# Combining a pair's two linear maps with two full-width products in place of four half-width ones

## The chip, the cores and the metric

The kernel runs on one core of a Trainium2 chip. The metric is device time in microseconds, the median of several runs. Before the change it is 644.4 us (three runs, 644.12 to 645.06).

## What is computed

For 128 samples, each a 128 x 2048 matrix `x[b]` in float32, two conditioned linear layers with residuals are applied one after the other. The weights of each layer are picked by an integer per sample:

```python
def _L0_cond_ref(x, weights, condition):
    return jnp.einsum('bct,bcd->bdt', x, weights[condition])          # 16 maps of 128x128

def _L1_cond_ref(x, subjects, weights, biases):
    out = jnp.einsum('bct,bcd->bdt', x, weights[subjects])            # 32 maps of 128x128
    return out + jnp.transpose(biases[subjects], (0, 2, 1))

x = x + _L0_cond_ref(x, L0_cond_weights, itok_B_0_15)
x = x + _L1_cond_ref(x, itok_B_0_31, L1_cond_weights, L1_cond_biases)
```

So each output is (I + W1)^T (I + W0)^T x + bias, and the two 128 x 128 maps can be multiplied into one before x is touched. x and the output are 134 MB each.

## The kernel before

Samples are taken in 64 pairs, k = 0 and 1 being the two samples of a pair. A sample's 128 rows lie on 64 partitions, two rows (u = 0 and 1) behind each other on a partition, so that sample 0 fills partitions 0 to 63 and sample 1 partitions 64 to 127, and a pair is one 2 MB transfer each way with 16 KB runs. `xt` has 8 slots of one pair each. Results are written back into the slot and stored from there.

**Queues.** SP issues the loads: the two weight tables, then the 64 pair loads (line 111), each of them from the ninth on waiting until the store of its slot has landed. ACT issues the 64 stores (line 262). These are the only large transfers.

**POOL** (lines 125 to 139) forms, for each sample, `map0T` = transposed W0 + I (line 137) and `map1` = W1 + I (line 138). Both tiles have two buffers, one per pair in turn; from pair 2 on POOL waits for the combining of two pairs before.

**PE** (lines 141 to 206). `combine` (line 151) multiplies the two maps of each sample of a pair: four products with 64 weight columns and 128 moving columns, for k = 0, 1 and u = 0, 1, which put sample k's result on partitions 64k to 64k + 63 of columns 1536 to 1791 of `acc1`, the first half of its last bank. `pair` then multiplies the combined map, copied to `both`, with x: 16 products (`term`, line 159) of 512 columns on 64 rows, alternately of sample 0 into `acc0` and of sample 1 into `acc1`, over four blocks j = 0 to 3 of 512 columns. The combining for the next pair is issued in the middle of a pair, between blocks 1 and 2; block 3 of `acc1` uses the bank in which the combined maps lie, and waits for `both_ready` before it. PE's program has the first eight pairs written out, then a loop over six groups of eight, then the last eight written out. Each float32 product is two matmul instructions and two weight loads in the trace.

**DVE** (lines 222 and 224) takes sample 0's results out of `acc0` with the bias added, in halves of 1024 columns, **ACT** (line 247, `odd_out`) sample 1's out of `acc1`. Between its first and second `odd_out` of a pair ACT does `copy_maps` for the next pair (line 240): one 128 x 256 copy of the combined maps to `both`. The order of ACT's work in a pair is: odd_out, copy_maps, odd_out, then two more odd_outs and the store's issue. PE waits for `lo_out0`, `lo_out1`, `hi_out0` and `hi_out1` (results taken out) before it writes the same banks for the next pair.

Of the kernel before, what the change touches and what calls it, by code (L numbers as in the profile page):

```python
# [5 lines left out]
def conditioned_residual_kernel(  # L6
# [12 lines left out]
    ALU = mybir.AluOpType  # L19
    ACT = mybir.ActivationFunctionType  # L20
    POOL = mybir.EngineType.Pool

    B, C, T = x.shape
    S0, S1 = w0T.shape[1], w1.shape[1]
    HC = C // 2
# [13 lines left out]
    with ctx:  # L39
        def sb(name, shape, dt=fp32):  # L40
            return ctx.enter_context(nc.sbuf_tensor(name, shape, dt))

        def pb(name, shape):
            return ctx.enter_context(nc.psum_tensor(name, shape, fp32))
# [15 lines left out]
        map0T = sb("map0T", [C, 2, 2, 2, HC])  # L60
        map1 = sb("map1", [C, 2, 2, 2, HC])
        both = sb("both", [C, 2, 2, C])
# [3 lines left out]
        acc1 = pb("acc1", [C, T])  # L66

        CB = T - CHUNK
# [16 lines left out]
        both_ready = sem("both_ready")  # L85
# [11 lines left out]
        w0T_v = w0T_sb[:, :, :].rearrange("p s (i u) -> p s u i", u=2)  # L97
        w1_v = w1_sb[:, :, :].rearrange("p s (i u) -> p s u i", u=2)
        ident_v = ident[:, :].rearrange("p (i u) -> p u i", u=2)
# [13 lines left out]
        @block.gpsimd  # L113
        def _(pool):
            nc.gpsimd.memset(ident[:, :], 0.0).then_inc(zeroed, 1)  # L115
            nc.gpsimd.iota(row[:, :], [[0, B]], base=0, channel_multiplier=1).then_inc(row_ready, 1)  # L116
            pool.wait_ge(zeroed, 1)
            nc.gpsimd.affine_select(out=ident[:, :], in_=ident[:, :], compare_op=ALU.not_equal, fill=1.0, base=0,  # L118
                                    pattern=[[-1, C]], channel_multiplier=1).then_inc(ident_ready, 1)
            pool.wait_ge(ident_ready, 1)  # L120
            pool.wait_ge(cond_loaded, LOAD)
            pool.wait_ge(w0_loaded, LOAD)
            pool.wait_ge(w1_loaded, LOAD)
            GROUP = 16
            for b in range(B):
                if b % GROUP == 0:
                    _, i0 = nc.values_load_multi_w_load_instructions(  # L127
                        cond_sb[0:1, 0, b:b + GROUP], engines=[POOL], min_val=0, max_val=S0 - 1,
                        skip_runtime_bounds_check_because="conditions index the maps")
                    _, i1 = nc.values_load_multi_w_load_instructions(  # L130
                        cond_sb[0:1, 1, b:b + GROUP], engines=[POOL], min_val=0, max_val=S1 - 1,
                        skip_runtime_bounds_check_because="conditions index the maps")
                q, k = b // 2, b % 2
                if q >= 2 and k == 0:

                    pool.wait_ge(combined, q - 1)
                nc.gpsimd.tensor_tensor(map0T[:, q % 2, k, :, :], w0T_v[:, bass.ds(i0[b % GROUP], 1), :, :], ident_v, ALU.add)  # L137
                nc.gpsimd.tensor_tensor(map1[:, q % 2, k, :, :], w1_v[:, bass.ds(i1[b % GROUP], 1), :, :], ident_v,  # L138
                                        ALU.add).then_inc(maps_ready, 1)

        @block.tensor
        def _(pe):

            pe.wait_ge(bias_loaded, LOAD)
            pe.wait_ge(ident_ready, 1)
            nc.tensor.matmul(acc0[0:S1, 0:C], bias_sb[:, :], ident[:, :], start=True, stop=True).then_inc(turned, 1)  # L146
            pe.wait_ge(onehot_ready, 1)
            pe.wait_ge(biasT_ready, 1)
            nc.tensor.matmul(acc1[:, 0:B], biasT[:, :, :], onehot[:, :], start=True, stop=True).then_inc(picked, 1)  # L149

            def combine(q, buf):
                pe.wait_ge(maps_ready, 2 * q + 2)
                for k in range(2):
                    for u in range(2):
                        last = nc.tensor.matmul(acc1[k * HC:(k + 1) * HC, CB + u * C:CB + (u + 1) * C],  # L155
                                                map0T[:, buf, k, u, :], map1[:, buf, k, :, :], start=True, stop=True)
                last.then_inc(combined, 1)

            def term(acc, k, u, buf, slot, j):
                return nc.tensor.matmul(acc[:, j * CHUNK:(j + 1) * CHUNK], both[k * HC:(k + 1) * HC, buf, u, :],  # L160
                                        xt[k * HC:(k + 1) * HC, slot, u * T + j * CHUNK:u * T + (j + 1) * CHUNK],
                                        start=u == 0, stop=u == 1)

            def pair(q, slot, turn, begins, ends):
                buf = slot % 2
                pe.wait_ge(x_loaded[slot], (turn + 1) * LOAD)
                pe.wait_ge(both_ready, q + 1)
                if not begins:
                    pe.wait_ge(lo_out0, q)
                term(acc0, 0, 0, buf, slot, 0)  # L170
                if not begins:
                    pe.wait_ge(lo_out1, q)
                term(acc1, 1, 0, buf, slot, 0)
                term(acc0, 0, 1, buf, slot, 0)
                term(acc1, 1, 1, buf, slot, 0)
                term(acc0, 0, 0, buf, slot, 1)
                term(acc1, 1, 0, buf, slot, 1)
                term(acc0, 0, 1, buf, slot, 1).then_inc(lo_done0, 1)
                term(acc1, 1, 1, buf, slot, 1).then_inc(lo_done1, 1)
                if not begins:  # L180
                    pe.wait_ge(hi_out1, q)
                if not ends:
                    combine(q + 1, 1 - buf)
                if not begins:
                    pe.wait_ge(hi_out0, q)
                term(acc0, 0, 0, buf, slot, 2)
                term(acc1, 1, 0, buf, slot, 2)
                term(acc0, 0, 1, buf, slot, 2)
                term(acc1, 1, 1, buf, slot, 2)
                term(acc0, 0, 0, buf, slot, 3)  # L190
                if not ends:

                    pe.wait_ge(both_ready, q + 2)
                term(acc1, 1, 0, buf, slot, 3)
                term(acc0, 0, 1, buf, slot, 3).then_inc(hi_done0, 1)
                term(acc1, 1, 1, buf, slot, 3).then_inc(hi_done1, 1)

            def group(turn, begins, ends):
                for s in range(SLOTS):
                    pair(turn * SLOTS + s, s, turn, begins and s == 0, ends and s == SLOTS - 1)  # L200

            pe.wait_ge(bias_ready, 1)
            combine(0, 0)
            group(0, True, False)
            with pe.Fori(1, TURNS - 1) as turn:
                group(turn, False, False)
            group(TURNS - 1, False, True)
# [25 lines left out]
        @block.scalar  # L233
        def _(act):
            act.dma_start(cond_sb[:, :, :], conds).then_inc(cond_loaded, LOAD)
            act.dma_start(bias_sb[:, :], bias1).then_inc(bias_loaded, LOAD)
            act.dma_start(cond_rep[:, :], conds[0:1, 1, :].to_broadcast([S1, B])).then_inc(rep_loaded, LOAD)
            act.wait_ge(bias_ready, 1)

            def copy_maps(q):  # L240

                act.wait_ge(combined, q + 1)
                nc.scalar.activation(both[:, q % 2, :, :], acc1[:, CB:CB + 2 * C], ACT.Identity).then_inc(both_ready, 1)  # L243

            def odd_out(q, v, a):

                return nc.scalar.activation(xt[HC:C, q % SLOTS, v * T + a:v * T + a + HALF], acc1[v * HC:(v + 1) * HC, a:a + HALF],  # L247
                                            ACT.Identity, bias=bias_of[v * HC:(v + 1) * HC, 2 * q + 1:2 * q + 2])

            copy_maps(0)  # L250
            for q in range(PAIRS):
                act.wait_ge(lo_done1, q + 1)
                odd_out(q, 0, 0)
                if q < PAIRS - 1:
                    copy_maps(q + 1)
                odd_out(q, 1, 0).then_inc(lo_out1, 1)
                act.wait_ge(hi_done1, q + 1)
                odd_out(q, 0, HALF)
                odd_out(q, 1, HALF).then_inc(hi_out1, 1)
                act.wait_ge(hi_out0, q + 1)  # L260
                act.wait_ge(hi_out1, q + 1)
                act.dma_start(out_pairs[q, :, :], xt[:, q % SLOTS, :]).then_inc(stored[q % SLOTS], LOAD)
            for q in range(SLOTS):
                act.wait_ge(stored[q], LOAD * TURNS)
# [27 lines left out]
```

## Time and profile before

| what | value |
|---|---|
| median of three runs | 644.4 us |
| profiled execution: own time / span | 643.72 us / 641.6 us |
| granted TensorE clock, mean | 0.964 |
| PE busy | 525.4 us (82%) |
| PE weight loads busy | 224.2 us (35%) |
| DVE, ACT, POOL busy | 329.2, 309.4, 124.1 us |
| DMA moved | 271.82 MB, mean 424 GB/s |

The own time is what the execution took on the device; the span goes from its first to its last instruction. "Busy" is the time in which at least one instruction of an engine ran. The clock is the share of full speed that TensorE was granted. The 271.82 MB are x in, the result out, and about 3.4 MB of weights, instructions and small tables. The page's row of DMA share in 40 slices reads 8 in the first slice, 9 (90% or more) in 38 and 5 in the last.

### The profile page before, as it was taken

The page shows a single profiled execution, that of the slowest core. Times are in us where ns is not written, and L with a number is a line of the kernel's source. Part 1 is how long each engine was busy: PE and PEld are TensorE (multiplying, and loading weights), DVE is VectorE, ACT ScalarE, POOL GpSimd, SP SyncE. Part 2 cuts the span into 40 slices and gives each one's busy share as a digit, 9 for nine tenths or more (in the row PEclk, how much of TensorE's full clock was granted, in tenths as well). Part 3 has the DMA queues.
Part 4 walks back from the last instruction along what each step waited for, and adds up shares of the span by engine and source line. Part 5 has one row for each costly group of instructions (what it writes and reads, how often), then busy time and mean ns, then how long its engine had stood idle before and what let it go on. Part 6 is the DMA issues. An engine that isn't in the chain of part 4 may idle for free.

```text
span 641.6 us, 6679 instructions
## 1 busy us (share of the span) xinstructions
PE 525.4 (82%) x2564; PEld 224.2 (35%) x2564; DVE 329.2 (51%) x259; ACT 309.4 (48%) x321; POOL 124.1 (19%) x263
## 2 busy tenths in 40 slices
PE   1899999887787787887888977889878888779880
PEld 0344443333333333333333433333333333334330
DVE  0366666455545544554546445455554545455450
ACT  0466665444544544544446445355454445454450
POOL 2222222121221221221212212122112122121000
PEclk9999999899999999999989899899999889998896
DMA  8999999999999999999999999999999999999995
GB/s 361 436 396 434 429 430 431 428 433 430 429 431 432 433 431 430 430 430 434 429 431 431 430 433 431 430 432 430 431 431 431 432 431 429 431 431 431 430 430 246
DMA packets 18931, 271.82 MB, mean 424 GB/s; under 512 B 2241, under 2 KB 2274, under 8 KB 2274
## 3 DMA queue, kind: packets, MB, share of 16 engines
q1 hardware_dynamic: 9504, 137.37, 50.3%
q10 hardware_dynamic: 9410, 134.26, 48.9%
q8 instruction: 7, 0.11, 0.1%
q14 instruction: 10, 0.08, 0.0%
HBM read 137.40 MB, written 134.22 MB: 423 GB/s over the span
## 4 chain that ended last, share of the span: by engine, by line
DMA 75%; PE 19%; DVE 3%; ACT 1%; POOLq 0%; issue 0%; DVEq 0%; POOL 0%; SPq 0%; ACTq 0%
DMA out_dram<-xt 40%; DMA xt<-in_x_dram 33%; PE acc L160 17%; PE acc L155 1%; DMA w_sb<-in_w_dram 1%; DVE xt L222 1%; DVE xt L224 1%; ACT xt L247 0%; DVEq L39 0%; ACT L243 0%; POOLq L127 0%; POOLq L130 0%; POOL map0T L137 0%; POOL map L138 0%; ACT both L243 0%
## 5 line engine op out<-in xcount | busy, mean ns | idle before, releaser
L160 PE MATMUL acc<-xt,both 64*128 64x512 f32 x2048 | 489.8, 621 | 85.2 <-DMA xt<-in_x_dram 83.2
L247 ACT ACTIVATE xt<-acc,bias_of 64x1024 f32<-64x1024 f32 x256 | 283.6, 1108 | 300.2 <-PE acc L160 297.8
L160 PEld LDWEIGHTS acc<-xt,both 64*128 64x128 f32 x2048 | 196.2, 193 | 336.7 <-issue 223.5
L222 DVE TENSOR_SCALAR xt<-acc,bias_of 64x1024 f32<-64x1024 f32 x128 | 163.3, 1276 | 282.1 <-PE acc L160 282.1
L224 DVE TENSOR_SCALAR xt<-acc,bias_of 64x1024 f32<-64x1024 f32 x128 | 165.1, 1290 | 1.9
L137 POOL TENSOR_TENSOR map0T<-w0T_sb,ident 128x128 f32<-128x128 f32 x128 | 65.6, 512 | 469.6 <-PE acc L155 457.8
L138 POOL TENSOR_TENSOR map<-w_sb,ident 128x128 f32<-128x128 f32 x128 | 65.7, 513 | 0.0
L155 PEld LDWEIGHTS acc<-map,map0T 128*64 128x64 f32 x512 | 27.4, 137 | 49.3 <-issue 48.1
L155 PE MATMUL acc<-map,map0T 128*64 128x128 f32 x512 | 43.0, 287 | 0.9 <-POOL map L138 0.9
L243 ACT ACTIVATE both<-acc 128x256 f32<-128x256 f32 x64 | 24.5, 383 | 0.8
L146 PE MATMUL acc<-ident,bias_sb 128*32 128x128 f32 x2 | 0.6, 422 | 10.7 <-DMA bias_sb<-in_bias_dram 10.7
L243 ACT ACT_TABLE_LOAD x1 | 1.3, 1283 | 16.4 <-PE acc L155 16.4
L213 DVE TENSOR_TENSOR onehot<-cond_rep,row 32x128 f32<-32x128 int32 x1 | 0.3, 280 | 12.9 <-DMA cond_rep<-in_conds_dram 12.9
L146 PEld LDWEIGHTS acc<-ident,bias_sb 128*32 128x32 f32 x2 | 0.2, 142 | 10.7 <-DMA bias_sb<-in_bias_dram 10.7
L149 PE MATMUL acc<-onehot,biasT 32*128 32x128 f32 x2 | 0.8, 480 | 2.2 <-DVE biasT L215 2.2
L149 PEld LDWEIGHTS acc<-onehot,biasT 32*128 32x128 f32 x2 | 0.5, 304 | 2.6 <-DVE onehot L213 2.6
L217 DVE COPY bias_of<-acc 128x128 f32<-128x128 f32 x1 | 0.3, 291 | 0.9 <-PE acc L149 0.9
L215 DVE COPY biasT<-acc 32x128 f32<-32x128 f32 x1 | 0.3, 279 | 0.0
L118 POOL TENSOR_SCALAR_AFFINE_SELECT ident<-ident 128x128 f32<-128x128 f32 x1 | 0.3, 282 | 0.0
L115 POOL MEMSET ident<- 128x128 f32 x1 | 0.2, 204 | 0.3 <-POOLq L281 0.3
L116 POOL IOTA row<- 32x128 int32 x1 | 0.2, 224 | 0.0
L281 POOL MEMSET const-float32-0.0<- 128x1 f32 x1 | 0.1, 98 | 0.2 <-issue 0.2
(3 smaller groups left out, 0.3 us busy)
## 6 DMA issues: line engine op xcount, KB each, us to landing
xt<-in_x_dram SPq DMA_DIRECT2D x64, 2048.0 KB, 30.7
out_dram<-xt ACTq DMA_DIRECT2D x64, 2048.0 KB, 37.2
w_sb<-in_w_dram SPq DMA_DIRECT2D x1, 2048.0 KB, 9.4
w0T_sb<-in_w0T_dram SPq DMA_DIRECT2D x1, 1024.0 KB, 4.8
cond_sb<-in_conds_dram ACTq DMA_DIRECT2D x1, 1.0 KB
bias_sb<-in_bias_dram ACTq DMA_DIRECT2D x1, 16.0 KB, 9.4
cond_rep<-in_conds_dram ACTq DMA_DIRECT2D x1, 16.0 KB, 11.1
```

The lines of the kernel that those rows point to most:

```text
L118: nc.gpsimd.affine_select(out=ident[:, :], in_=ident[:, :], compare_op=ALU.not_equal, fill=1.0, base=0, pattern=[[-1, C]], channel_multipl ...
L137: nc.gpsimd.tensor_tensor(map0T[:, q % 2, k, :, :], w0T_v[:, bass.ds(i0[b % GROUP], 1), :, :], ident_v, ALU.add)
L138: nc.gpsimd.tensor_tensor(map1[:, q % 2, k, :, :], w1_v[:, bass.ds(i1[b % GROUP], 1), :, :], ident_v, ALU.add).then_inc(maps_ready, 1)
L146: nc.tensor.matmul(acc0[0:S1, 0:C], bias_sb[:, :], ident[:, :], start=True, stop=True).then_inc(turned, 1)
L149: nc.tensor.matmul(acc1[:, 0:B], biasT[:, :, :], onehot[:, :], start=True, stop=True).then_inc(picked, 1)
L155: last = nc.tensor.matmul(acc1[k * HC:(k + 1) * HC, CB + u * C:CB + (u + 1) * C], map0T[:, buf, k, u, :], map1[:, buf, k, :, :], start=Tru ...
L160: return nc.tensor.matmul(acc[:, j * CHUNK:(j + 1) * CHUNK], both[k * HC:(k + 1) * HC, buf, u, :], xt[k * HC:(k + 1) * HC, slot, u * T + j ...
L213: nc.vector.tensor_tensor(onehot[:, :], cond_rep[:, :], row[:, :], ALU.is_equal).then_inc(onehot_ready, 1)
L222: nc.vector.tensor_scalar(xt[0:HC, q % SLOTS, a:a + HALF], acc0[0:HC, a:a + HALF], bias_of[0:HC, 2 * q:2 * q + 1], None, ALU.add)
L224: return nc.vector.tensor_scalar(xt[0:HC, q % SLOTS, T + a:T + a + HALF], acc0[HC:C, a:a + HALF], bias_of[HC:C, 2 * q:2 * q + 1], None, AL ...
L243: nc.scalar.activation(both[:, q % 2, :, :], acc1[:, CB:CB + 2 * C], ACT.Identity).then_inc(both_ready, 1)
L247: return nc.scalar.activation(xt[HC:C, q % SLOTS, v * T + a:v * T + a + HALF], acc1[v * HC:(v + 1) * HC, a:a + HALF], ACT.Identity, bias=b ...
```

## The change

`combine` makes two products in place of four. Each has 128 weight columns (both samples' rows of one u, side by side) and 256 moving columns (both samples' columns). The result has four blocks, of which the two crossed ones (rows of one sample with columns of the other) are not used. It fills all 512 columns of `acc1`'s last bank. `map0T` is laid out with u ahead of k for it, so line 137 writes two separate runs of 64 columns. `copy_maps` copies the two wanted blocks, sample 0's from partitions 0 to 63 and sample 1's from partitions 64 to 127, in two instructions of 64 partitions x 256 elements. The wait at a pair's start for `both_ready` is left out except in the very first pair; the wait ahead of block 3 of the pair before covers it.

```diff
-                nc.gpsimd.tensor_tensor(map0T[:, q % 2, k, :, :], w0T_v[:, bass.ds(i0[b % GROUP], 1), :, :], ident_v, ALU.add)
+                nc.gpsimd.tensor_tensor(map0T[:, q % 2, :, k, :], w0T_v[:, bass.ds(i0[b % GROUP], 1), :, :], ident_v, ALU.add)
...
             def combine(q, buf):
+
                 pe.wait_ge(maps_ready, 2 * q + 2)
-                for k in range(2):
-                    for u in range(2):
-                        last = nc.tensor.matmul(acc1[k * HC:(k + 1) * HC, CB + u * C:CB + (u + 1) * C],
-                                                map0T[:, buf, k, u, :], map1[:, buf, k, :, :], start=True, stop=True)
+                for u in range(2):
+                    last = nc.tensor.matmul(acc1[:, CB + u * 2 * C:CB + (u + 1) * 2 * C],
+                                            map0T[:, buf, u, :, :], map1[:, buf, :, :, :], start=True, stop=True)
                 last.then_inc(combined, 1)
...
                 pe.wait_ge(x_loaded[slot], (turn + 1) * LOAD)
-                pe.wait_ge(both_ready, q + 1)
-                if not begins:
+                if begins:
+                    pe.wait_ge(both_ready, 1)
+                else:
+
                     pe.wait_ge(lo_out0, q)
...
                 act.wait_ge(combined, q + 1)
-                nc.scalar.activation(both[:, q % 2, :, :], acc1[:, CB:CB + 2 * C], ACT.Identity).then_inc(both_ready, 1)
+                crossed = acc1[:, CB:T].rearrange("p (u k c) -> p u k c", u=2, k=2)
+                nc.scalar.activation(both[0:HC, q % 2, :, :], crossed[0:HC, :, 0, :], ACT.Identity)
+                nc.scalar.activation(both[HC:C, q % 2, :, :], crossed[HC:C, :, 1, :], ACT.Identity).then_inc(both_ready, 1)
```

## Rows read from the trace of the kernel before

**Rows 1.** Windows: stretch, length; busy us (instructions) per engine; clock, DMA share, GB/s.

```profile
14.00:84.00 70.00, 67.21 (x344) 30.39 (x345) 41.16 (x33) 40.18 (x42) 20.23 (x43) 1.00 1.00 423
150.00:540.00 390.00, 326.27 (x1584) 138.01 (x1586) 204.66 (x160) 192.03 (x200) 77.13 (x160) 0.97 1.01 431
```

**Rows 2.** The chain that ended last, whole span: shares, then pieces (start, us, what).

```profile
by line: DMA out_dram<-xt 39.7%; DMA xt<-in_x_dram 33.4%; PE acc L160 17.1%; PE acc L155 1.5%; DMA w_sb<-in_w_dram 1.5%; DVE xt L222 1.4%; DVE xt L224 1.2%; issue 0.4%; ACT xt L247 0.3%; DVEq L39 0.2%; ACT L243 0.2%; POOLq L127 0.2%; POOLq 
...
15.23 1.14 PE acc L155 x8
...
23.71 0.59 PE acc L155 x8
24.31 7.07 PE acc L160 x32
...
84.27 31.18 DMA out_dram<-xt
```

**Rows 3.** Stores issued in 30:31, 84:85 and 627:628, last number us to landing.

```profile
out_dram<-xt ACTq DMA_DIRECT2D x1, 2048.0 KB, 15.9
...
out_dram<-xt ACTq DMA_DIRECT2D x1, 2048.0 KB, 31.2
...
out_dram<-xt ACTq DMA_DIRECT2D x1, 2048.0 KB, 14.0
```

**Rows 4.** Waits (total us, times, longest): first of 84:560, second of 14:84.

```profile
PE acc L160 <- DMA xt<-in_x_dram: 75.2, 46, 2.4
...
PE acc L160 <- ACT both L243: 1.9, 1, 1.9
```

**Rows 5.** Groups by line: busy, mean ns, then idle before, with its releaser.

```profile
L155 PE MATMUL acc<-map,map0T 128*64 128x128 f32 x512 | 43.0, 287 | 0.9 <-POOL map L138 0.9
```

**Rows 6.** Timeline 28:46, a pair that PE paces: start, us, instruction, idle before.

```profile
31.30 0.66 PE L155 MATMUL acc<-map,map0T 128*64 128x128 f32 x8
...
31.45 1.11 ACT L247 ACTIVATE xt<-acc,bias_of 64x1024 f32<-64x1024 f32 x1 [1.20 <-PE acc L160]
...
32.17 0.51 POOL L137 TENSOR_TENSOR map0T<-w0T_sb,ident 128x128 f32<-128x128 f32 x1 [5.74 <-PE acc L155]
32.57 0.38 ACT L243 ACTIVATE both<-acc 128x256 f32<-128x256 f32 x1
...
32.98 1.11 ACT L247 ACTIVATE xt<-acc,bias_of 64x1024 f32<-64x1024 f32 x1
...
35.68 2.23 ACT L247 ACTIVATE xt<-acc,bias_of 64x1024 f32<-64x1024 f32 x2 [1.59 <-PE acc L160]
```

**Rows 7.** Timeline 0:30, around the first pair's start.

```profile
17.74 0.38 ACT L243 ACTIVATE both<-acc 128x256 f32<-128x256 f32 x1
...
18.27 5.44 PE L160 MATMUL acc<-xt,both 64*128 64x512 f32 x16 [1.91 <-ACT both L243]
```

**Rows 8.** Timeline 605:645, the last pair: its products and its store's issue.

```profile
617.32 7.14 PE L160 MATMUL acc<-xt,both 64*128 64x512 f32 x32 [1.95 <-DMA xt<-in_x_dram]
...
627.10 0.34 ACTq L262 DMA_DIRECT2D out_dram<-xt  x1
```

**Rows 9.** DMA queues (packets, MB, share): the page; 88:89; 150:540; 635.9:641.6.

```profile
q8 instruction: 7, 0.11, 0.1%
...
q8 instruction: 1, 0.02, 6.0%
...
q14 instruction: 6, 0.05, 0.0%
...
q10 hardware_dynamic: 8, 0.11, 4.7%
```

**Rows 10.** Windows between two instruction fetches, and from the last of them on.

```profile
562.40:591.80 29.40, 25.39 (x122) 10.60 (x120) 15.28 (x13) 14.33 (x16) 5.77 (x12) 0.94 1.01 430
...
591.80:626.00 34.20, 28.63 (x134) 11.84 (x130) 19.18 (x16) 17.88 (x19) 1.93 (x4) 0.95 1.01 431
```

## The prediction

> **What bounds the kernel now.** I read the windows first [rows 1]. The reader is to see the last two columns: from 14 to 84 us the share of the 16 DMA engines is 1.00 at 423 GB/s, from 150 to 540 us 1.01 at 431 GB/s. There is no stretch in the body in which the transfers stand still. PE is busy for 326 of the 390 us, but that is no bound: in the same stretch its 1584 products are 39.6 pairs of 40 (32 of line 160, 8 of line 155), so a pair takes 390 / 39.6 = 9.85 us, and a pair is 4.19 MB, which at 431 GB/s is 9.73 us. PE needs only 0.59 + 7.07 = 7.66 us for a pair when nothing holds it [rows 2], and 9.85 - 7.66 = 2.19 us per pair are over. Where they go the waits show: PE stands 75.2 us for loads of x between 84 and 560 us, and no other wait of PE's data on another engine is in that list; POOL, DVE and ACT wait for PE [rows 4, 6].
>
> The chain of waits, read second, seems to say otherwise for the start: 17.1% of it is line 160 and 1.5% line 155, because from 15 to 84 us it runs through PE alone, a combining of 0.59 us and then 7.07 us of products, pair after pair, into the store issued at 84.27 us, which takes 31.18 us to land [rows 2]. The third view settles which is right: the store issued at 30.6 us takes 15.9 us to land, the one at 84.3 us 31.2 us [rows 3]. Alone, 2.1 MB at 430 GB/s would be 4.9 us. So 11 us of other transfers stand ahead of or beside the first store, and 26 us beside the eighth: already while PE sets the pace, a backlog of transfers grows. The end of the run is the end of the bytes: total bytes over a rate that is always used. A PE or ACT cost shows in the time only if it empties this backlog, or if it lies behind the last load.
>
> **The products.** Removed: four products of 64 weight columns by 128 moving columns, eight instructions, 0.59 us from start to the next line's start [rows 2, 5]. Added: two products with 128 weight columns by 256 moving columns, four instructions, if float32 is still split in two. What one costs: line 160 does 32 instructions of 512 columns in 7.07 us, two at a time on the two halves of the rows, so a step of 512 columns is 7.07 / 16 = 0.44 us [rows 2], and 256 columns 0.22 us. I assume that nothing runs beside a product that takes the whole array, so 4 x 0.22 = 0.88 us: +0.29 us a pair. Ends: below, two of them beside each other, 0.44 us (-0.15); above, at half the clock, 1.76 us (+1.17), since the first pair's first half takes 5.44 us in place of 3.7 although the column of the clock reads 1.00 [rows 1, 7]. I take +0.29 us, by the nearest row at speed. It is hidden by the 2.19 us for which PE waits for loads; even the upper end fits. With the cover gone it would be 63 x 0.29 = 18 us.
>
> The Trainium skill speaks against this edit. TensorEngine Tiling (Array Packing), section Key Properties, has different tiles execute weight loads and products in parallel, so the old form, in 64-column tiles, could overlap its two samples, and the new one can't. The trace agrees in part: eight instructions of 128 columns one by one would be 8 x 0.11 = 0.88 us, and they take 0.59. By the rule at its fullest the old form would be 0.44 us and the change +0.44 us a pair; the sum is the same, since that too is under the 2.19 us.
>
> **The copies.** Removed: one 128 x 256 copy of 0.38 us. Added: two of 64 x 256, as many elements on each partition. From the start of the old copy to the next instruction's start is 32.98 - 32.57 = 0.41 us [rows 6], so I take 0.41 each: +0.41 us. Ends: nothing gained or lost beneath 0 (half the partitions for half the price, +0), and above the 1.11 us of the 64 x 1024 activation on the same partitions (+1.11 - 0.41 = 0.70 more). Queued behind it on ACT is the pair's second odd_out, whose end lets PE begin the next pair in acc1: it would end at 32.98 + 0.41 + 1.11 = 34.50 us, and ACT's next work comes at 35.68 [rows 6]. 1.2 us are over, and the upper end fits too. PE waits for the copies itself ahead of block 3 of acc1: it gets there one combining and four steps of 0.44 us after the combining's start, 31.30 + 0.88 + 1.77 = 33.95 us, with the weight load one step sooner, 33.5 us. The copies begin when odd_out ends (32.57, with the combining long done at 31.30 + 0.88 = 32.18) and end at 32.57 + 0.41 + 0.38 = 33.36 us. So 0.15 us are over; by the upper end PE would lose some 0.6 us a pair, and 0.6 + 0.29 is still under 2.19 us. By +1.17 and +0.6 together it would be 1.8 us, just under.
>
> **POOL's line 137** writes two runs in place of one. It costs 0.51 us, and POOL stands idle for 5.74 us before each pair even when PE paces [rows 6]; between +0 and twice the price, +1.0 us a pair, it is hidden.
>
> **The wait left out** goes with one that stays (block 3 of the pair before waits for the same copies). PE never stood at a pair's start for these maps except at 18.27 us [rows 4, 7], which wait stays. 0 us, and at most one instruction less a pair.
>
> **The head.** The combining for pair 0 takes 1.14 us there [rows 2]; times 0.88 / 0.59 it is 1.70, +0.56 us. The second copy adds 0.41, so pair 0 begins 1.0 us later. Eight combinings with +0.29 us follow by 84 us: the eighth store is issued 1.0 + 2.3 = 3.3 us later. What hides it is the backlog, 11 us at the first store and more at each later one [rows 3]. With all upper ends together the delay would be 1.0 + 8 x 1.8 = 15 us at the eighth store, where the backlog is 26.
>
> **The tail.** After the last load landed (617.3 us) the last pair has no combining and no copy; it takes 7.14 us of products, its store is issued at 627.10 and lands 14.0 us later [rows 3, 8]. Its own 4.9 us of bytes are the smaller part of that: the queue is full to the end. Untouched: 0.
>
> **Instruction fetches** are a term of their own, because the very end belongs to one DMA engine. Between 635.9 and 641.6 us only 8 packets move, one behind the other, 4.7% of 16 engines [rows 9]: fifteen engines are done, and one is some 5 us late. Equal shares of x lie on all, so it had other work. The queue q8 brought 7 packets of 16 KB, at 6.0% of 16 engines in 1 us, 0.96 us each [rows 9]; 7 x 0.96 = 6.7 us is about the lateness, if they lie on this engine, which the trace doesn't name. They fit PE's program: one comes with every 122 + 120 = 242 products and weight loads [rows 10], and none between 150 and 540 us, where PE loops and only q14 fetches [rows 9]. The change takes 8 of a pair's 80 such instructions away, 24 times in the program as written, 192 in all, and up to 24 waits. After the last of the seven fetches 134 + 130 = 264 are left [rows 10]. 264 - 192 - 24 = 48: the seventh fetch moves toward the end but still comes, in the last pair. So 0 us, with -0.96 if it falls away. ACT gets 64 instructions more, at most one more of q14's packets, which are 8 KB (0.05 MB for 6), half the size: +0.5 us as the upper end, 0 taken.
>
> The Trainium skill, Runtime: NRT & Kernel Launch, section Instruction fetch mechanics, says that a refill brings 256 instructions and that a taken branch out of a two-page window forces a fetch. The first half agrees with the 242 (waits not counted). By the second half each of the loop's turns would fetch, and a shorter body would save some; the trace shows no packet of q8 in five turns, so the trace decides and the sum has no such term.
>
> **Sum.** 641.6 us of span + 0 = 641.6; own time 643.72 + 0. The median of the runs shown is 0.7 us above that own time, so I forecast the median itself, **644.4 us**.
>
> **Rivals.**
> A. One fetch of PE's program falls away, and the late engine's end with it: 644.4 - 0.96 = 643.4 us. For it: the margin is only 48 instructions. Against: it is positive, and other steps than these may set the late engine. 0.12.
> B. More than that comes off the late engine (two fetches, or the packets fall more evenly): 644.4 - 1.9 = 642.5 us, the faster case. Nothing in the count speaks for two. 0.05.
> C. The head sets the end, as the chain of waits shows it, because the backlog runs dry when the stores come later: 644.4 + 3.3 = 647.7 us. It decides from the point where a store's delay is over the 11 us of other transfers beside the first store [rows 3]. Against: 3.3 us is far under that, and the share is 1.00 from 14 us on [rows 1]. This is the slower case. 0.05.
> D. The products don't come out as I think (split otherwise, or at half the clock) and PE needs up to 1.8 us more a pair. Under 2.19 us the time stays 644.4; 0.06. It would be slower only beyond: each 0.1 us over that is 6 us. 0.02.
> My forecast as it stands: 0.70.
>
> **How the numbers follow.** A measurement of this kernel can tell about 0.2%, 1.3 us, from no change: 643.1 to 645.7. The forecast, A and the first part of D lie inside, 0.87 (0.01 of A falls under 643.1). Faster: that and B, 0.06. Slower: C and the second part of D, 0.07. The range reaches down past A to 643.2, and up by the 0.66 us by which the highest of the runs shown lies over the median and the 0.5 us of q14, rounded, to 645.4.
>
> **What would show each step.** Line 155 with 256 matmul instructions in place of 512, 0.88 us from a combining's start to the next products; if 0.6, the old form gained nothing from its tiles. Two copies at line 243, 0.41 us apart. PE's wait for loads of x down by about 0.29 us a pair, some 14 us over 84:560, and the pair still 9.85 us. The store at 30.6 us issued 1 to 1.6 us later, and the eighth some 3 us later and landing in less time than 31.2 us, at the same 46.5 and 115.5 us or so. q8 with 7 packets before the end, the last near 618 us. The forecast is wrong if the DMA share falls under 1 anywhere between 14 and 634 us, or if PE waits for ACT's copies in the loop by over 1.5 us a pair.

## The result: 1.85 us faster, and the profile after

The kernel after takes 642.49 us (8 runs, 642.28 to 643.22), the kernel before in the same comparison 644.34 us (8 runs, 643.42 to 645.06): a ratio of 0.9973, 95% interval 0.9964 to 0.9981. A second timing of the unchanged kernel after, on another chip, gave 642.70 us and 0.9980 (0.9969 to 0.9990). I had forecast 644.4 us, range 643.2 to 645.4; the measured median lies under that range.

First the page of the kernel after; groups by line have busy us, mean ns, then idle before. They answer to the table of before and to [rows 5].

```profile
span 641.1 us, 6225 instructions
...
L160 PE MATMUL acc<-xt,both 64*128 64x512 f32 x2048 | 471.7, 602 | 70.6 <-DMA xt<-in_x_dram 68.2
...
L155 PE MATMUL acc<-map,map0T 128*128 128x256 f32 x256 | 73.3, 409 | 0.9 <-POOL map L138 0.9
...
L247 ACT ACTIVATE both<-acc 64x256 f32<-64x256 f32 x64 | 24.2, 378 | 0.7
L246 ACT ACTIVATE both<-acc 64x256 f32<-64x256 f32 x64 | 24.1, 377 | 0.7
```

The instruction count fell from 6679 to 6225: 512 of PE's away, 64 of ACT's more, and the wait's register work. Line 155 has 256 matmul instructions, as foreseen. The mean granted TensorE clock is 0.989, against 0.964 before, and one instruction of line 160 takes 602 ns on average, against 621.

The timeline of a pair that PE paces, against [rows 6] (start, us, instruction, idle before):

```profile
32.27 0.36 ACTq L266 DMA_DIRECT2D out_dram<-xt  x1
...
32.99 1.13 PE L155 MATMUL acc<-map,map0T 128*128 128x256 f32 x4
...
34.05 7.14 PE L160 MATMUL acc<-xt,both 64*128 64x512 f32 x32
34.25 0.38 ACT L246 ACTIVATE both<-acc 64x256 f32<-64x256 f32 x1
34.30 0.51 POOL L137 TENSOR_TENSOR map0T<-w0T_sb,ident 128x128 f32<-128x128 f32 x1 [6.20 <-PE acc L155]
...
34.64 0.38 ACT L247 ACTIVATE both<-acc 64x256 f32<-64x256 f32 x1
...
35.04 1.11 ACT L251 ACTIVATE xt<-acc,bias_of 64x1024 f32<-64x1024 f32 x1
```

The combining takes 34.05 - 32.99 = 1.06 us from its start to the next products', against 0.59 [rows 2]. The two copies start 0.39 us apart. POOL's line 137 takes 0.51 us as before. PE's pair is 1.06 + 7.07 = 8.13 us, against 7.66 [rows 2]. So PE became slower, and the kernel faster.

Windows (busy us and counts of PE, weight loads, DVE, ACT, POOL; clock, DMA share, GB/s) and the wait for loads in 84:560, against [rows 1, 4]:

```profile
14.00:84.00 70.00, 66.85 (x284) 30.68 (x285) 38.34 (x31) 40.40 (x49) 19.26 (x41) 1.00 1.01 426
150.00:540.00 390.00, 333.20 (x1431) 142.80 (x1427) 202.65 (x158) 204.83 (x237) 75.47 (x157) 1.00 1.01 431
```

```profile
PE acc L160 <- DMA xt<-in_x_dram: 59.6, 42, 1.5
```

The transfers run at the same 431 GB/s; PE waits 59.6 us for loads in place of 75.2, as its slower pair eats into that idle time. (The combining's 0.47 us more in some 49 pairs would be 23 us; the long products, faster at the higher clock, give part of it back.) The chain of waits gives PE even more of the span than before, in pieces of 7.07 us up to the ninth combining, and the eighth store, issued at 89.17 us in place of 84.27, lands after 27.0 us in place of 31.2 [rows 2, 3]:

```profile
by line: DMA out_dram<-xt 42.1%; DMA xt<-in_x_dram 29.6%; PE acc L160 17.1%; PE acc L155 2.6%; DVE xt L224 1.6%; DMA w_sb<-in_w_dram 1.5%; DVE xt L226 1.4%; issue 0.3%; DVEq L39 0.2%; ACT L246 0.2%; POOLq L127 0.2%; POOLq L130 0.2%; POOL ma
...
89.17 26.99 DMA out_dram<-xt
```

It lands at 116.2 us, before 115.5: of a delay of 4.9 us, 4.2 were absorbed by the backlog. Nothing in the middle of the run tells of a gain. The end does. DMA queues (packets, MB, share) of the page, and of 635.9:641:

```profile
q8 instruction: 7, 0.11, 0.1%
...
q10 hardware_dynamic: 7, 0.10, 4.5%
```

Again one engine alone moves the last packets, one behind the other, after the other fifteen are done.

**How late this engine is, and since when.** Each transfer of x ends with 16 small completion packets, one for each DMA engine. The packets' records in the trace hold the start of each; they don't name the engine, so "the sixteenth" below is the one that completes last. For every load I took how much later the last of its 16 completions came than the first; the rows of the 15th give the same for the last but one:

```
load landing near (us)     94    211    327    444    561    last data packet ends
before, last behind first  2.1   2.7    3.9    5.4    6.8    640.7
after                      1.9   2.2    3.5    4.7    6.0    640.1 (span 641.1)
the 15th, before           2.1   2.5    2.5    2.5    2.5    635.7
the 15th, after            1.4   1.9    1.9    2.3    2.6    635.5
```

The first completions of the loads come 9.725 us apart in both kernels, and the other fourteen engines stay near the first. The sixteenth falls back a little with every pair from the start on; a line through the loads that land between 280 and 600 us gives 116.5 ns a pair before and 102.4 after. Over 65 pairs that is 14 x 65 = 0.9 us. A second trace of the unchanged kernel before gave 135.0 ns a pair, second and third traces of the kernel after and of a near copy 100.8 and 100.6, so the difference is 14 to 34 ns, 0.9 to 2.2 us, and the 1.85 us lie inside. The time between span and own time is 1.8 us in nearly all runs of all kernels, so the gain isn't there. Over the 15 traces without the last store and the 32 memsets of the table below, the last data packet ends the later the steeper this slope is: 638.7 us at 92 ns, 639.4 to 640.1 at 101 to 102, 641.4 to 641.7 at 135 to 137, with a correlation of 0.95 and a rise of 0.056 us for each ns a pair, what 56 of the 64 pairs would give.

This lateness also sets PE's pair. A load is there for PE when its last completion has come, so PE's pair is 9.725 + 0.116 = 9.84 us before and 9.725 + 0.102 = 9.83 after. The chains of waits show it in the starts of PE's products eight pairs apart, first before (78.7 us), then after (78.6 us):

```profile
459.87 3.70 PE acc L160 x16
...
538.58 3.70 PE acc L160 x16
```

```profile
457.72 3.70 PE acc L160 x16
...
536.32 3.70 PE acc L160 x16
```

**Where the lateness comes from, packet by packet.** A data packet of 16 KB is recorded with 611 ns. Between 150 and 540 us some 11 of a pair's 256 are recorded a little longer, mostly by 1 to 30 ns, and these additions sum to 109 ns a pair before and 101 after, near the two slopes. I cut the stretch into slots of 607 ns and counted the instructions that end in each:

```
instructions that end in the slot        0     1-4   5-8   9-12  13 and more
mean addition in ns, before              2.2   3.7   7.3   9.5   15.2 (44 slots)
after                                    1.5   4.3   6.8   8.8   10.3 (7 slots)
after + 24 PE instructions a pair        4.7   7.2   6.0   7.1   17.9 (55 slots)
```

The additions fall where many instructions end; in all 17 traces the two are correlated, by 0.22 to 0.43. Of the 44 crowded slots before, 39 hold the old combining, whose eight products and eight weight loads run within 0.66 us; the new combining makes no such slot. If these packets are the late engine's, as their sum suggests, this shows when it is held up, though not by what.

### The profile page after: what moved, and what is told of

Same layout as the page of the kernel before. It is cut to its first block, busy times and chain, and to the rows that moved or that the text cites. A ratio compares the mean times of both kernels' runs of the same rounds, so it can differ in the third digit from the quotient of the medians.

```text
span 641.1 us, 6225 instructions
## 1 busy us (share of the span) xinstructions
PE 537.6 (84%) x2308; PEld 234.0 (37%) x2308; DVE 329.2 (51%) x259; ACT 333.2 (52%) x385; POOL 123.9 (19%) x263
## 4 chain that ended last, share of the span: by engine, by line
DMA 73%; PE 20%; DVE 3%; POOLq 0%; issue 0%; ACT 0%; DVEq 0%; POOL 0%; SPq 0%; ACTq 0%
DMA out_dram<-xt 42%; DMA xt<-in_x_dram 30%; PE acc L160 17%; PE acc L155 3%; DVE xt L224 2%; DMA w_sb<-in_w_dram 1%; DVE xt L226 1%; DVEq L39 0%; ACT L246 0%; POOLq L127 0%; POOLq L130 0%; POOL map0T L137 0%; POOL map L138 0%; ACT both L247 0%; ACT both L246 0%
## 5 line engine op out<-in xcount | busy, mean ns | idle before, releaser
L160 PE MATMUL acc<-xt,both 64*128 64x512 f32 x2048 | 471.7, 602 | 70.6 <-DMA xt<-in_x_dram 68.2
L160 PEld LDWEIGHTS acc<-xt,both 64*128 64x128 f32 x2048 | 189.5, 187 | 321.5 <-issue 224.1
L155 PE MATMUL acc<-map,map0T 128*128 128x256 f32 x256 | 73.3, 409 | 0.9 <-POOL map L138 0.9
L155 PEld LDWEIGHTS acc<-map,map0T 128*128 128x128 f32 x256 | 43.8, 191 | 52.3 <-issue 47.8
L247 ACT ACTIVATE both<-acc 64x256 f32<-64x256 f32 x64 | 24.2, 378 | 0.7
L246 ACT ACTIVATE both<-acc 64x256 f32<-64x256 f32 x64 | 24.1, 377 | 0.7
```

The source lines that it names most:

```text
L155: last = nc.tensor.matmul(acc1[:, CB + u * 2 * C:CB + (u + 1) * 2 * C], map0T[:, buf, u, :, :], map1[:, buf, :, :, :], start=True, stop=True)
L246: nc.scalar.activation(both[0:HC, q % 2, :, :], crossed[0:HC, :, 0, :], ACT.Identity)
L247: nc.scalar.activation(both[HC:C, q % 2, :, :], crossed[HC:C, :, 1, :], ACT.Identity).then_inc(both_ready, 1)
```

## The experiments

All times are medians, with the ratio of the run to the kernel before on the same chip (the ratios go nearly by the means, so they and the medians can differ by 0.1%; the medians of the kernel before on the four chips are 644.1 to 644.3 us). "ns a pair" is the slope just described, of one profiled execution each; it scatters by some 20 ns for old-form kernels.

```
kernel                                    us       ratio, 95% interval       instr.  ns a pair
before, again                             643.64   0.9990 (0.9980, 0.9999)   6679    135.0
two copies alone                          644.52   1.0001 (0.9992, 1.0009)   6743    136.5
wait left out alone                       643.41   0.9989 (0.9980, 0.9998)   6673    137.4
two products and copies, wait kept        642.63   0.9976 (0.9966, 0.9986)   6231    100.6
after                                     642.49   0.9973 (0.9964, 0.9981)   6225    102.4
after, again                              642.70   0.9980 (0.9969, 0.9990)   6225    100.8
after + 8 PE instructions a pair          643.60   1.0000 (0.9990, 1.0009)   6737    117.8
after + 24 PE instructions a pair         643.93   1.0005 (0.9993, 1.0018)   7761    119.6
after + 8 DVE instructions a pair         643.70   0.9994 (0.9984, 1.0003)   6737    120.7
after + 32 DVE instructions a pair        652.74   1.0135 (1.0115, 1.0154)   8273    -
after, half of x's products               641.67   0.9958 (0.9944, 0.9973)   4177    92.3
before, PE's loop written out             643.94   0.9997 (0.9987, 1.0006)   6606    112.9
before, half of the combining products    643.50   0.9988 (0.9980, 0.9997)   6175    107.4
before, maps formed for two pairs only    643.53   0.9991 (0.9977, 1.0004)   6169    101.6
the same, again                           643.63   0.9989 (0.9981, 0.9998)   6169    127.0
after, last store cut in two              646.57   1.0034 (1.0022, 1.0047)   6226    104.4
```

### Which part of the change

The kernel before, against itself:

> The kernel before, unchanged, timed against itself. Every theory expects a ratio of 1.000 with an interval of about 0.1% on both sides; the point is to see how far the spans of its executions scatter and how much of a time lies outside the span (2.1 us in the profiled execution of before, 1.8 us in that of after).

0.9990 with an interval that just leaves 1 out. So a single ratio here can't be trusted to better than 0.1%, 0.6 us; the gain of 0.27% is clear of that, a third of it isn't. The spans of the kernel before run from 641.1 to 643.9 us over some 30 executions, those of the kernel after from 640.4 to 641.4 with one at 643.5.

The two copies alone:

```diff
-                nc.scalar.activation(both[:, q % 2, :, :], acc1[:, CB:CB + 2 * C], ACT.Identity).then_inc(both_ready, 1)
+                nc.scalar.activation(both[0:HC, q % 2, :, :], acc1[0:HC, CB:CB + 2 * C], ACT.Identity)
+                nc.scalar.activation(both[HC:C, q % 2, :, :], acc1[HC:C, CB:CB + 2 * C], ACT.Identity).then_inc(both_ready, 1)
```

> The kernel before with its one 128x256 copy of the combined maps made as two of 64x256; four products and all waits as before. Theory F (the gain comes from PE's shorter program: its instruction fetches, which share the DMA engine that ends last): no gain, 644.3 us, ratio 0.999 to 1.001, and q8 fetches at the same times as before. Theory T (the later and more even rhythm of ACT's work, and with it the stores, gives the gain): most of the 1.85 us, 642.5 to 643.0 us.

644.52 us: no gain. Theory T fell.

The wait left out alone:

```diff
-                pe.wait_ge(both_ready, q + 1)
-                if not begins:
+                if begins:
+                    pe.wait_ge(both_ready, 1)
+                else:
                     pe.wait_ge(lo_out0, q)
```

> The kernel before with the wait for both_ready at a pair's start left out in all but the first pair. Theory F: at most one instruction a pair less on PE, 24 in its program, so at most a small part: 643.9 to 644.4 us. Theory W (the wait left out is the gain): 642.5 us. Theory T: 644.3 us.

0.9989, the same as before against itself: nothing that can be told from no change.

The kernel after with that wait put back (the same lines the other way round):

> The kernel after with the wait for both_ready at a pair's start put back: two products and two copies remain. Theory F: nearly the whole gain, 642.5 to 642.9 us, since 192 of PE's instructions stay away. Theory W: 644.3 us. Theory T: 642.5 us.

642.63 us, the whole gain. It goes with the two products; the wait isn't needed for it, and neither the copies nor the wait alone are enough. (Two products without the two copies weren't run; the new layout asks for both.)

### Is it PE's program, fetched?

The kernel before with PE's loop written out:

```diff
-            with pe.Fori(1, TURNS - 1) as turn:
-                group(turn, False, False)
+            for turn in range(1, TURNS - 1):
+                group(turn, False, False)
```

> The kernel before with PE's loop written out: the same products and waits, but 5 x 8 pairs x 83 = 3320 more instructions in the program, 13 more packets of 16 KB on q8 at 0.96 us. Theory F, all of q8 on the engine that ends last: 644.3 + 12.5 = 656.8 us. If q8's packets are spread over the engines: under 645.1 us. Theory N: the instructions executed fall by some 170 (the loop's register work), 643.6 us, plus whatever theory F adds.

643.94 us. The queue of the fetches in 150:540 (no packet before, [rows 9]):

```profile
q8 instruction: 13, 0.21, 0.2%
```

Thirteen packets more, and no time. In the completions the reason is seen: one time this engine, the next time that one falls back by 0.6 to 0.7 us, until eight of them are 2.8 to 5 us behind the first, and the engine that ends last is none the later (112.9 ns a pair, last data at 640.5 us). PE's fetches are spread over the engines. That struck out the term on which my count of the end was built.

DVE's are not. The kernel after with memsets on DVE, eight or 32 of one column behind the first output of every pair:

```diff
                 even_out(q, 0).then_inc(lo_out0, 1)
+                for i in range(32):   # 8 in the smaller one
+                    nc.vector.memset(spare[:, 32 * q + i:32 * q + i + 1], 0.0)
```

> The kernel after with eight memsets of one column each on DVE behind the first output of every pair, 512 instructions more on an engine that waits 280 us for PE. Theory N with any engine's instructions alike: 642.5 + 2.1 = 644.6 us. Theory N with PE's alone: 642.5 us. Theory F: 512 instructions are four packets of 8 KB (0.31 us each) on q14: 643.7 us if all lie on the late engine.

643.70 us. The second latest engine fell back in jumps of 0.85 us, some 104 us apart (q14's packets at 241.4, 348.6, 452.2 and 556.4 us), which is DVE's rhythm of 128 instructions at 12 a pair; the latest went on smoothly, at 120.7 ns a pair. This jump sized the next:

> The kernel after with 32 memsets of one column on DVE a pair, 2048 instructions more, all in DVE's program. Theory N, proportional: 102 + 32 x 1.1 = 137 ns a pair on the late engine, 2.3 us, 644.8 us. Theory N, flattening as with 24 more on PE: 643.9 us. Besides, q14 would fetch DVE's program in 16 more packets; with eight memsets a pair the second latest engine fell back by 0.86 us with each of DVE's fetches, so with 32 this engine would fall back by 16 x 0.86 = 14 us and end last: 635 + 2.8 + 14 = 652 us.

652.74 us, against 652 worked out. The page's span, DVE's group and queue, then the windows 635:641 and 643:649:

```profile
span 650.0 us, 8273 instructions
...
q14 instruction: 26, 0.21, 0.1%
...
L234 DVE MEMSET spare<- 128x1 f32 x2048 | 30.9, 59 | 0.6 <-issue 0.2
```

```profile
635.00:641.00 6.00, 0.00 (x0) 0.00 (x0) 0.52 (x1) 0.21 (x1) 0.00 (x0) 0.73 0.84 360
643.00:649.00 6.00, 0.00 (x0) 0.00 (x0) 0.00 (x0) 0.00 (x0) 0.00 (x0) 0.50 0.07 30
```

The memsets cost DVE 30.9 us in all, 0.5 us a pair, far under its idle time; what costs 10 us is 16 packets of 8 KB more on q14. From 644.3 us on one engine alone still stores (0.07 of 16 is one engine): its last data packet ends at 649.2 us, where fourteen others had ended by 641.5. That the engine which ends last sets the time, with all others done, is shown by this one most plainly. The fourteen themselves ended some 6 us later than in the kernel after (635.5); I put that down to the loads, which land only when the slowest engine has brought its rows, so that stores start later. No run tests this alone. The small additions to the packets sum to 141 ns a pair here.

### Is it the number of instructions executed, or the form of the product?

Tiny products of 32 weight columns by one moving column ahead of each combining, two or six of them:

```diff
                 pe.wait_ge(maps_ready, 2 * q + 2)
+                for _ in range(2):   # 6 in the larger one
+                    nc.tensor.matmul(acc1[0:32, CB:CB + 1], map0T[:, buf, 0, 0, 0:32], map1[:, buf, 0, 0, 0:1], start=True, stop=True)
```

> The kernel after with two tiny extra products ahead of each combining (32 weight columns by one moving column, 8 instructions, overwritten by the real ones): PE executes and holds about as many instructions as in the kernel before, in the new form of the product. Theory N (one DMA engine carries a small load that grows with the number of instructions executed; it is the engine whose packets end last): back to 644.0 to 644.5 us, and the lag of this engine behind the others grows by some 4.5 us between 190 and 540 us, in place of 3.8. Theory M (the full-width product itself, its time or its clock, is the gain): 642.5 us as the kernel after.

> The kernel after with six tiny extra products ahead of each combining, 24 instructions a pair, 1536 in all. Theory N, by 1.85 us for the 454 instructions that the change took away (4 ns each): 642.5 + 6.3 = 648.8 us. Theory F (only fetched program counts: 24 x 24 = 576 instructions more in the program, two and a quarter packets of 16 KB): 642.5 + 2.2 = 644.7 us. Theory M: 642.5 us, as long as PE's pair stays under 9.85 us.

643.60 and 643.93 us. The two groups of tiny products, first of the smaller one, then of the larger:

```profile
L155 PE MATMUL acc<-map,map0T 128*32 128x1 f32 x256 | 18.4, 175 | 0.7 <-POOL map L138 0.7
```

```profile
L155 PE MATMUL acc<-map,map0T 128*32 128x1 f32 x768 | 34.7, 172 | 0.8 <-POOL map L138 0.8
```

With as many instructions as before, 1.1 of the 1.85 us are gone, in the new form of the product, at the same high granted clock (0.989) as after; by the ratio, 1.0000, the whole gain is gone. So theory M, the form or the clock alone, falls. But three times the addition takes only 0.3 us more, and 119.6 ns a pair: proportional, as I had written it (648.8 us), the effect is not. Theory F's 644.7 us for this one falls too, as after the written-out loop it must. Eight on DVE (643.70 us) did the same as eight on PE.

The other direction, a kernel with half of x's products left out:

```diff
-                term(acc0, 0, 1, buf, slot, 0)
-                term(acc1, 1, 1, buf, slot, 0)
...
-                                        start=u == 0, stop=u == 1)
+                                        start=True, stop=True)
```

> The kernel after with the products of u = 1 left out (half of the sum over x's rows is missing): 32 instructions fewer a pair, 64 in place of 96. PE's pair falls to some 4.4 us, the transfers are the same. Theory N: the late engine falls back by about 64 x 1.1 = 70 ns a pair in place of 102, 65 x 0.032 = 2.1 us less at the end: 640.4 us. Any theory in which instructions don't count: 642.5 us. The floor is where the other engines end, 635 us plus 2.8 us, 637.9 us.

641.67 us and 92.3 ns a pair: faster, though by 0.8 us against after in place of 2.1, and at a lower granted clock (0.857). PE waits 198 us for loads in it:

```profile
L160 PE MATMUL acc<-xt,both 64*128 64x512 f32 x1024 | 320.9, 742 | 200.4 <-DMA xt<-in_x_dram 198.1
```

Fifteen engines end at 635.4 us, as in the kernel after (635.5); the sixteenth ends at 638.7 in place of 640.1. So it is again this engine that makes the difference.

Then as many instructions away as the change takes, in the old form, once on PE and once on POOL:

```diff
-                for k in range(2):
+                for k in range(2 if isinstance(q, int) and q == 0 else 1):
```

> The kernel before, old half-width form, with sample 1's two combining products left out in all pairs but the first (sample 1 gets wrong maps): 8 PE instructions fewer a pair, 504 in all, as the change takes away. Theory N (the number of executed instructions loads one DMA engine steadily): 642.4 to 642.8 us, late engine 100 to 104 ns a pair behind. Theory M (the full-width form is the gain): 644.2 us, 116 to 137 ns.

```diff
-            for b in range(B):
+            for b in range(4):
...
-                if q >= 2 and k == 0:
-                    pool.wait_ge(combined, q - 1)
...
-                pe.wait_ge(maps_ready, 2 * q + 2)
+                pe.wait_ge(maps_ready, 4)
```

> The kernel before with its four half-width products, but POOL forms the maps of the first two pairs only, and all pairs are combined from these two buffers (the weights of the later samples are left out, so the output is another one). Some 500 instructions fewer are executed, on POOL in place of PE. Theory N (a steady load on one DMA engine that follows the number of executed instructions of any engine): as the kernel after, 642.3 to 642.7 us, and this engine falls back by some 100 ns a pair in place of 116 to 137. Theory M (the full-width product is the gain) or N with PE's instructions alone: 644.1 us.

> The kernel before without POOL's map forming after pair 1 again, since its first 12 runs spread from 641.95 to 645.93 us. Theory N with any engine's instructions: 642.4 to 642.8 us. Theory N with PE's alone, or M: 644.2 us.

643.50, 643.53 and 643.63 us, ratios of 0.9988 to 0.9991: each lower than before, none clearly by more than before against itself (0.9990), and all about 1 us above the kernel after. So fewer instructions in the old form give at most half of the gain, where the theory asked for all of it. The slopes, 107.4, 101.6 and 127.0 ns, contradict each other; a single trace is too little for a difference of 20 ns.

> The kernel after, unchanged, again, on the chip of the other three. Every theory: 642.5 us, late engine 100 to 104 ns a pair behind. If it comes out over 643.4 us, the gain of 1.85 us is in part a matter of chip or hour.

642.70 us: the gain itself stands, on a chip on which these did not reach it.

### Taking bytes off the late engine

```diff
+                if q < PAIRS - 1:
+                    act.dma_start(out_pairs[q, :, :], ...)
+            q = PAIRS - 1
+            act.dma_start(out_pairs[q, 0:120, :], xt[0:120, q % SLOTS, :]).then_inc(stored[q % SLOTS], LOAD)
+            act.dma_start(out_pairs[q, 120:128, :], xt[120:128, q % SLOTS, :]).then_inc(stored[q % SLOTS], LOAD)
```

> The kernel after with the last pair's store cut in two: rows 0 to 119, which by the Trainium skill (DMA: Bandwidth & Descriptors, Why a DMA increments its semaphore by 16 and not by 1) lie on 15 of the 16 engines, and rows 120 to 127 on 8. If the late engine is the sixteenth, it has 8 packets fewer at the end, 8 x 0.607 = 4.9 us, and the time is 642.5 - 4.9 + what the two transfers cost, 637.6 to 638.5 us. If it is one of the other fifteen: 642.5 to 643.7 us.

646.57 us, worse than either case that I had written. Windows 627:638 and 638:645:

```profile
627.00:638.00 11.00, 0.00 (x0) 0.00 (x0) 0.00 (x0) 0.00 (x0) 0.00 (x0) 0.50 0.78 270
638.00:645.00 7.00, 0.00 (x0) 0.00 (x0) 0.00 (x0) 0.00 (x0) 0.00 (x0) 0.50 0.06 26
```

The last engine ends some 4 us later than in the kernel after, its last packet at 644.3 us in place of 640.1. Its records stand end to end: eight packets from 638.87 us, a completion, one more packet, a completion. So the engine that ends last has its share of the 120 rows and one packet of the other eight; it isn't the one that a store of 120 rows leaves out. The records count 15 + 8 completions for the two stores, as the Trainium skill has it on the page DMA: Bandwidth & Descriptors, section Why a DMA increments its semaphore by 16 and not by 1. The second store's packet is 0.6 us of the delay. The rest came before: of the data packets that start after 624 us, 37 took 0.7 to 2.6 us in place of 0.61, together 26 us more than at 0.611 us each, and none did so in the kernel after. So this store in two parts is itself slower, why isn't known, and the run can't tell what fewer bytes on the late engine would have given. Which version would relieve the late engine stays open; no kernel that beats the one after and computes the same was found.

## Why the prediction was wrong

**Right.** The bound: transfers, full from start to end, with PE's and ACT's costs hidden. The combining was mis-sized (1.06 us against 0.88, so +0.47 us a pair in place of +0.29), and the eighth store came 4.9 us later in place of 3.3. The two cost nothing, as argued, by PE's idle time and by the backlog. Rival C, the head's chain of waits, had its delay and more, and the time fell: the chain was no bound there. The copies (0.39 us apart for 0.41), POOL's 0.51 us, q8's seven packets before the end: as forecast, the last at 610 us in place of 618. PE's wait (15.6 us less for "some 14") agrees in part by luck: the combining took more than forecast, and the granted clock rose from 0.964 to 0.989, which I hadn't forecast, and made the long products faster.

**The step that failed** is the one headed instruction fetches. I had seen that the end belongs to one DMA engine, some 5 us late, and put its lateness down to "the queue q8 brought 7 packets of 16 KB", 7 x 0.96 = 6.7 us, "if they lie on this engine, which the trace doesn't name". They don't: 13 more of them cost no time, and seven in both kernels went with 1.85 us of difference. The lateness grows by 100 to 137 ns with every pair, also from 150 to 540 us, where there is no packet of q8 [rows 9]; I had that row, and should have asked whether the lateness grows there. The trace did hold the answer, in the completions, before any run. So did my first paragraph, with 9.85 us for a pair and 9.73 us for its bytes: the 0.12 us between them is what the sixteenth engine loses with every pair, and "total bytes over a rate that is always used" describes the other fifteen, which end 5 us sooner. What came was rival B, "more than that comes off the late engine", 642.5 us, to which I gave 0.05 since "nothing in the count speaks for two" fetches. Its size was right by luck, for its mechanism, fetches, was not what happened.

**What takes their place.** Shown: the engine that ends last sets the time; it falls back steadily; in the kernels with the two products it does so by less; neither the copies nor the wait alone bring the gain, and it stays when the wait is put back; 512 instructions put back on PE or on DVE bring back 1.1 to 1.2 us of the 1.85 by the medians; packets are stretched most where many instructions end, in sum by as much as that engine falls back. Not shown: what the steady load on that engine is. It rises with the instructions executed, but not in proportion (in the new form 92, 102, 118 to 121, 120 ns for 65, 97, 105, 121 instructions a pair), and taking 504 of them away in the old form gave 0.8 us at most. Number and crowding seem to act together, and the old combining was the most crowded place; that is argued, not shown. One rival stands untested: every timed execution has a span and a granted clock on record, so the profiler recorded all of them, and the load may be its own record of each instruction. No run here was timed without it.

## What to carry to other kernels

A kernel whose transfers are always full is not therefore deaf to its instructions: it ends when the latest of the 16 DMA engines ends, and here this one was 5 us behind the rest. Look at the last microseconds of the DMA share, and at the completions of each transfer over time: here a lag that grew smoothly was a steady load, and one that jumped was fetched program. If a pair takes longer than its bytes at the measured rate, even by 1%, ask what takes the difference. In such a kernel unrolled instructions on DVE can cost more than their run time (2048 memsets, 31 us of idle DVE time, 10 us at the end), and fewer, larger products can pay even when they take PE longer. How much of this is left without a profiler isn't known.

## What the runs showed of the hardware that I had not expected

- One DMA engine falls behind by 92 to 137 ns with every 4.19 MB, about 1% of its time, in all 16 traces for which the slope could be taken; the first completions come 9.725 us apart in all but the one with half of x's products (9.729).
- The lateness is made of small additions: some 9 to 12 data packets a pair are recorded over 611 ns, mostly by 1 to 30 ns, and most of all where many instructions end.
- PE's instruction fetches (16 KB, 0.9 us each) fell on changing engines; DVE's (8 KB, 0.31 us in the record) on one and the same, and each put it back by 0.85 us, more than twice its record.
- Four half-width combining products, eight instructions of 128 columns, took 0.59 us; two full-width ones, four of 256 columns, 1.06 us. At 0.44 us for 512 columns I had worked out 0.88.
- A tiny product of one moving column was recorded with 172 to 175 ns.
